# An unread 240-column product behind every four tiles of the degree and node-maximum products

## The reference, cut to what matters

```python
# layer 0: attention over the edges that end at a node
logit = (e_f @ W_a + b_a)[:, 0]
m = jax.lax.stop_gradient(jax.ops.segment_max(logit, edge_dst, num_segments=N))
ex = jnp.exp(logit - m[edge_dst])
den = jax.ops.segment_sum(ex, edge_dst, num_segments=N)
alpha = ex / den[edge_dst]
z_f = jax.ops.segment_sum(alpha[:, None] * n_f[edge_src], edge_dst, num_segments=N)
# layer 1: weights summed by source and by destination, and the number of edges of each
w_out = jax.ops.segment_sum(edge_w, src, num_segments=n)
deg_out = jnp.clip(jax.ops.segment_sum(ones, src, num_segments=n), 1.0)
```

## Time and profile before

| what | us |
|---|---|
| median of 3 executions | 601.23 |
| lowest, highest | 596.1, 601.38 |
| the profiled execution, its own time | 599.89 |
| its span, first to last instruction | 597.4 |
| outside the span | 2.5 |
| mean granted TensorE clock | 0.945 |

### The profile page before, as it was taken

One profiled execution on the slowest core, in us unless ns is written; L12 is line 12 of the kernel. 1 busy time (PEld: TensorE's weight loads), 2 busy tenths in 40 slices (PEclk: granted clock), 3 DMA queues, 4 the chain that ended last, 5 costly groups with the idle time before them and its releaser, 6 DMA issues.

```text
span 597.4 us, 7438 instructions
## 1 busy us (share of the span) xinstructions
PE 545.9 (91%) x2425; PEld 355.8 (60%) x2425; DVE 418.6 (70%) x744; ACT 214.3 (36%) x283; POOL 172.4 (29%) x163
## 2 busy tenths in 40 slices
PE   3999999999999998996399996898889999989996
PEld 2888888444444443432245454775657888868885
DVE  6999632588798789693986887666665276976234
ACT  3523434899455521000101192022524163224200
POOL 4014140477655735643473500000000001121000
PEclk9999999999999999899599995669997999989999
DMA  8956891899999999999799980040000656104002
GB/s 329 388 221 211 273 379 75 293 410 410 411 411 415 410 407 414 411 410 410 258 394 407 410 328 36 25 155 2 2 2 21 261 179 208 36 1 140 1 35 106
DMA packets 43492, 144.81 MB, mean 242 GB/s; under 512 B 5536, under 2 KB 5728, under 8 KB 43456
## 3 DMA queue, kind: packets, MB, share of 16 engines
q1 hardware_dynamic: 22000, 69.22, 31.0%
q0 software_dynamic: 19136, 69.22, 29.8%
q10 hardware_dynamic: 2320, 5.90, 2.6%
HBM read 131.70 MB, written 12.62 MB: 242 GB/s over the span
## 4 chain that ended last, share of the span: by engine, by line
PE 67%; DVE 16%; DMA 7%; issue 5%; POOL 1%; DVEq 1%; ACT 1%; ACTq 0%
PE banks L1089 23%; PE banks L1109 18%; PE banks L1251 7%; PE banks L1184 6%; DVE masked L796 4%; PE banks L1155 4%; PE banks L1268 4%; PE banks L1202 3%; DMA lift<-lift_row 3%; DVE rows L774 3%; DMA rows<-table,ids_i 2%; DVE rows L775 2%; DMA lift_row<-liftT 2%; DVE stats L676 1%; PE banks L1218 1%
## 5 line engine op out<-in xcount | busy, mean ns | idle before, releaser
L448 POOL DMA_INDIRECT rows<-table,ids_i x124 | 139.7, 1126 | 142.5 <-DVE rows L775 57.3
L1109 PE MATMUL banks<-w_raw,fT_raw 128*128 128x512 f32 x384 | 168.3, 599 | 7.6 <-DMA w_raw<-in_L_gnn_W_hn_dram 4.3
L1109 PEld LDWEIGHTS banks<-w_raw,fT_raw 128*128 128x128 f32 x384 | 73.0, 191 | 102.2 <-issue 89.4
L774 DVE TENSOR_TENSOR rows<-rows 128x1024 f32<-128x1024 f32 x62 | 75.7, 1222 | 35.3 <-DMA rows<-table,ids_i 27.8
L1089 PE MATMUL banks<-w_hi,fT_hi 128*128 128x512 f32 x200 | 78.1, 391 | 0.0
L686 DVE TENSOR_TENSOR w_lo<-w_raw,w_hi 128x1024 fp32r<-128x1024 f32 x40 | 48.3, 1224 | 42.2 <-ACT w_hi L497 37.1
L1089 PE MATMUL banks<-w_lo,fT_hi 128*128 128x512 f32 x200 | 77.8, 389 | 0.0
L1089 PE MATMUL banks<-w_hi,fT_lo 128*128 128x512 f32 x200 | 77.8, 389 | 0.0
L775 DVE SCALAR_TENSOR_TENSOR rows<-rows,wa_rep 128x1024 f32<-128x1024 f32 x62 | 75.9, 1225 | 2.1
L497 ACT ACTIVATE w_hi<-w_raw 128x1024 fp32r<-128x1024 f32 x40 | 41.7, 1056 | 78.3 <-PE banks L1089 63.8
L566 ACT ACTIVATE pick_src<-node_all,ids_f 128x512 f16<-128x512 f16 x64 | 42.7, 714 | 68.9 <-issue 34.5
(11 more groups left out here) (165 smaller groups left out, 643.7 us busy)
## 6 DMA issues: line engine op xcount, KB each, us to landing
w_raw<-in_L_gnn_W_ho_dram SPq DMA_DIRECT2D x16, 512.0 KB
table<-stage SPq DMA_DIRECT2D x32, 256.0 KB
w_raw<-in_L_gnn_W_oo_dram SPq DMA_DIRECT2D x16, 512.0 KB
w_raw<-in_L_gnn_W_on_dram SPq DMA_DIRECT2D x16, 512.0 KB
w_raw<-in_L_gnn_W_hn_dram SPq DMA_DIRECT2D x16, 512.0 KB
w_raw<-in_L_gnn_W_hh_dram SPq DMA_DIRECT2D x16, 512.0 KB
w_raw<-in_L_gnn_W_dram SPq DMA_DIRECT2D x8, 512.0 KB
lift<-lift_row ACTq DMA_DIRECT2D x7, 512.0 KB
```

Of the source, the lines that this page charges most:

```text
L448: pool.indirect_dma_start(out=rows[:, slot, side, :], out_offset=None, in_=table[kind][side], in_offset=bass.IndirectOffsetOnAxis(ap=ids_i ...
L774: step(dve.tensor_tensor(rows[:, r, 0, :], rows[:, r, 0, :], rows[:, r, 1, :], ALU.add))
L1109: ins = pe.matmul(bank[j][:, :], fT_raw[:, k, m * P:(m + 1) * P], w_raw[:, c % SLOTS, n * H:(n + 1) * H], start=(k == 0), stop=(k == K - 1))
```

## The change

A new function `keep_busy` makes one product of 240 columns: weights `zeros`, moving operand the first 240 columns of `node_all`, result in columns 192 to 431 of bank 7. Nothing reads that result, and nothing else lies there. It waits for nothing and signals nothing. It is called after every fourth tile in `degrees` and after every fourth tile but the last in `node_maxima`. TensorE's other instructions and those of all other engines stay as they are.

```diff
@@ -1158,6 +1158,10 @@
                         ins.then_inc(bank_done, 1)
                 ins.then_inc(chunk_used, 1)
 
+            def keep_busy():
+
+                pe.matmul(bank[7][:, 4 * P - 320:4 * P - 80], zeros[:, :], node_all[:, 0:240], start=True, stop=True)
+
             def degrees(tiles, opens=False, closes=False):
 
                 regions = bank[6][:, 0:4 * B]
@@ -1167,6 +1171,8 @@
                     for s in range(B):
                         pe.matmul(bank[6][:, 4 * s:4 * s + 4], pick_src[:, q, s * P:(s + 1) * P], w_col[:, q, :],
                                   start=False, stop=True, skip_group_check=True)
+                    if q % 4 == 3:
+                        keep_busy()
                 if closes:
                     pe.matmul(regions, zeros[:, :], node_no[:, 0:4 * B], start=False, stop=True,
                               skip_group_check=True).then_inc(deg_done, 1)
@@ -1217,6 +1223,8 @@
                     for b in range(B):
                         ins = pe.matmul(bank[7][:, 3 * t:3 * t + 3], member[:, b, t * P:(t + 1) * P].bitcast(F8),
                                         mpart[:, b, :], start=(b == 0), stop=(b == B - 1))
+                    if t % 4 == 3 and t < T - 1:
+                        keep_busy()
                 ins.then_inc(me_done, 1)
```

## The result

The changed kernel took 603.98 us in the median of 20 executions (598.48 to 608.36), the kernel before 597.94 us in the median of 20 (594.28 to 601.82). The ratio is 1.0079 with a 95% interval of 1.0054 to 1.0105, so the change costs 4.7 us (3.2 to 6.3). A ratio leaves out executions that lie over 1.5% above the fastest of their kernel, one of the 20 here, so it need not be the quotient of the medians. The medians are 6.0 us apart and the means 5.4 us. Both kernels scatter by 7 to 10 us from one execution to the next, more than the effect itself. The profiled execution of the changed kernel took 606.38 us. Its span, 604.4 us, is 7.0 us longer than that of the profiled execution of before, more than the mean difference.

A forecast was written before the change was run, and what follows sets the result against it. The prediction took the kernel to be bound by a chain running 67% through TensorE, partly at a low clock. Its terms, 0 + 0 + 3.0 + 0 us, on 599.89 us gave 602.9 us, range 598.4 to 605.8.

The forecast's parts named there:

- The price of one product: One added 240-column product on TensorE, from the spacing of 512-column ones: 0.202 us at the low clock, 0.101 at the high.
- The overlap: Added products on TensorE overlap with their neighbours, so each costs the spacing price, 0.202 us at the low clock.
- the upper bound of 0.38 us: Price of an added product on TensorE that overlaps with nothing, 0.38 us.
- The last 15: Products added in node_maxima, on the chain without cover, at the low clock: 3.0 us, bounds 1.5 and 5.7.
- The first 12: Products added in the first degrees group: 1.8 us, covered by TensorE's wait of 1.81 us for pick_src, so 0 us.
- The next 4: Products added in the second degrees group: 0.4 us before a wait of 1.18 us for the maxima's last part, so 0.
- What comes back by the clock: Clock falls before or during the maxima, three slow spans follow as before: 0 us, bounds one span (2.0 us) either way.
- back sooner: Rival: clock falls, but returns one span earlier behind the maxima; +1.0 us, 600.9 us, chance 0.20.
- held: Rival: added products keep the clock high through the maxima (ending at T); gain 3.6 us, time 596.3, chance 0.08.
- The sum: Whole kernel: 0 + 0 + 3.0 + 0 = 3.0 us on the profiled 599.89 us, giving 602.9 us.

The follow-up runs named there:

- the kernels with 31 and 63: Against the kernel before, 240-column products only in the maxima: behind every two tiles (31), 606.06 us, ratio 1.011; behind every tile but the last (63), 611.87 us, 1.0223.
- the maxima were dealt out: Against the kernel before, no added products; maxima's products in portions behind spans 3 to 9, exponents and split later: 598.46 us, ratio 0.9994.
- the two kernels that shortened it: Against the kernel before: maxima in portions behind spans, ratio 0.9994; eight unread 512-column products behind span 0, ratios 0.9965 and 1.0013.

## Why the prediction was right, and where its sizes were off

The forecast was 602.9 us, 3.0 us over its base, slower but within 1%. Measured are 603.98 us and +4.7 us (3.2 to 6.3). The total lies nearer to the forecast than the difference does, because the forecast stood on an execution of 599.89 us, 2 us above the kernel's median of 597.94. That the total is only 1.1 us off is luck.

**The price of one product** was right: 0.202 and 0.101 us predicted, 0.19 to 0.20 and 0.08 to 0.10 us in the spacing, and 0.21 us per product in the kernels with 31 and 63. The overlap was the right choice; the upper bound of 0.38 us does not apply to a queue of products. Nor does the figure for an isolated product, 382 ns, from the Trainium skill, "TensorE: Matmul & The Clock Gate", section "Single matmul latency"; the record of a single added product at the low clock, 0.36 us, is near it.

**The last 15**: predicted 10.0 us for the group and 0.50 for its clock; it was 9.77 us, with the clock at 1.00 for a first microsecond and 0.50 after. This step carries the result. The wait of VectorE was predicted at 6.2 us and is 8.47 us, of which 2.8 us are the group; the rest is that TensorE arrived later at the maxima in this execution.

**The first 12**: 0 us predicted, 1.0012 (0.9975 to 1.0048) measured alone. Their inner working was wrong in one point: the clock was taken to fall in the middle of the group as before, and in the changed kernel's trace it held to its end, so they cost 12 x 0.10 us there, all of it in front of a wait. The group lasted 6.2 us, where 6.5 to 7.5 was foretold. As the point of the fall differs between traces, with and without the twelve, it was no fixed input. The forecast's start of span 1 at 367.7 us was missed (369.35), since the group's end at 360.6 still lay 2.1 us before ScalarE's last piece. In this execution it was the upstream work that was late.

**The next 4**: 0 us predicted because of a cover of 1.18 us. That cover, 1.2 us, stands in the seven traces whose clock was high by the fold behind span 1, and in none of the other seven. In the changed kernel's profile the maxima start at 383.52 with no wait ahead of them, so these four, 0.4 us, lay on the path there. Reading a cover from a single trace was the weak step.

**What comes back by the clock**: 0 us with 2.0 us either way. The clock did fall, and three slow spans followed, as forecast. The price of 2.0 us for each slow span was somewhat oversized, and what "back sooner" would give was put too high. It counted TensorE's time alone, 4.21 less 2.24 us, or 0.5 us for each microsecond at the low clock. The two traces of before differ behind the maxima by 1.55 us for 2 x (0.24 x 32.62 - 0.19 x 31.07) = 3.9 us of low clock, 0.4 us for each. And an early return did not last: it was lost again in all seven traces that have one. In "held", the start of the products of span 11 at T + 17.2 does not follow from its own steps either, which come to T + 16.7 to 16.9. Over 76 executions of the kernel before, in the first three sets of the experiments, an execution with 1 us more at the low clock was only 0.29 us longer (slope of a straight line through them). This slope compares executions and is no price of a cause: where the maxima were dealt out, 12 us less of low clock came with no shorter time.

**The sum**: 3.0 us was the group alone. The measured 4.7 us leaves 1.7 us, 0.2 to 3.3. Two contributions can be named. The four late products cost up to 0.4 us where their cover is gone. And in the mean of the 20 executions TensorE was 70 us at the low clock against 63 in those 76 of before, of which the longer group explains 3; the other 4 us at 0.29 make 1.1 us. That is arithmetic and not a cause, and the kernel with 63 products has nothing beyond its group (75 us at the low clock, 13 over the kernel before beside it, for a group that is 12.6 us longer). Why the changed kernel, like the ones with 15 products or 120 tiny ones in the maxima (69 to 70 us), stays low for longer is open. The experiments show only that the twelve products in the first group alone do not make it longer (63 us), and that 240 streamed columns do not make it shorter than tiny products of the same length do.

## What to carry to other kernels

Filler on the path is a delay: before adding unread products to keep a clock up, ask what the engine behind them is waiting for, and put them where it waits, if anywhere. What a slow stretch costs is not the difference of the slow and the fast row but what remains when the partner engine becomes the bound: here 0.3 to 0.4 us for each microsecond at the low clock, by the comparison of executions and traces, with no gain measured in the two kernels that shortened it, and an early return was not even kept. Where executions differ by 1% among themselves, a cover or a clock state read from one trace is one draw, and needs a second trace before it stands as a term of 0.

## What the hardware showed that was not expected

TensorE was busy without a gap, with 63 products of 240 columns among 256 tiny ones, and the granted clock stayed at 0.50 for 19.4 us; one span of six 512-column products right behind, 2.4 us, and it was back. In the trace of before it took three such spans. The Trainium skill's page "TensorE: Matmul & The Clock Gate", Part 1, ties the clock to how busy the engine was and warns of gaps; here there was no gap, and these rows do not agree with busy time, as the profile counts it, being the measure. Products with weights of nothing but zeros seem to count as work. In both traces of the kernel with eight such products behind span 0 they ran at the high clock, the eight of 512 columns in 2.05 and 1.91 us, and the clock stayed high through the wait of 1.67 or 1.74 us behind them, until the wait for the maxima's parts. In three traces without them (the second of before, the second with the 15 in the maxima, the one with the tiny products) it was also high for a while behind span 0, but low again as span 1 began.

```profile
367.70 2.05 PE L1230 MATMUL banks<-node_all,zeros 128*128 128x512 f16 x8
371.41 1.28 PE L1184 MATMUL banks<-pick_src,pick_dst 128*120 x5 [1.67 <-DVE span_end L897]
```

These readings rest on one or two traces each.
